# Local attention on one Trainium2 core: the mask added in four 64x64 quarter products, and the queries' copy moved ahead of the cosine product

## The reference, cut to what matters

```python
h = shift_token(x)                       # half of the channels come from the token before
q, k, v = split(h @ wqkv, 3)             # 8 heads of 64
q, k = rotary_xpos(l2norm(q) * qs, l2norm(k) * ksc)
# windows of 64 queries; each sees its own 64 keys and the 64 before them
sim = einsum('bhwid,bhwjd->bhwij', q * 8, look_around(k))
sim = where((i < j) | (i > j + 64) | (j == -1), -max, sim)
out = softmax(sim) @ look_around(v)
x = x + out @ wo                         # then a gated feed-forward layer
```

## Time and profile before

| what | value |
|---|---|
| three runs, us | 3756.16, 3765.66, 10150.55 (median 3765.66) |
| the profiled execution, us | 3774.12 |
| its span from first to last instruction, us | 3772.3 |
| mean granted TensorE clock | 0.903 |
| PE busy in the span | 2956.8 us (78%) |
| DVE, ACT, POOL busy | 2501.2, 1754.1, 1870.5 us |
| stretches of local attention, from the span's start, us | 1538 to 1807, 1929 to 2199, 2994 to 3264, 3388 to 3657 |

### The profile page before, as it was taken

One profiled execution on the slowest core, in us unless ns is written; L12 is line 12 of the kernel. 1 busy time (PEld: TensorE's weight loads), 2 busy tenths in 40 slices (PEclk: granted clock), 3 DMA queues, 4 the chain that ended last, 5 costly groups with the idle time before them and its releaser, 6 DMA issues. The chain is left out here.

```text
span 3772.3 us, 66671 instructions
## 1 busy us (share of the span) xinstructions
PE 2956.8 (78%) x21951; PEld 1709.8 (45%) x21951; DVE 2501.2 (66%) x4010; ACT 1754.1 (46%) x3307; POOL 1870.5 (50%) x1303
## 2 busy tenths in 40 slices
PE   3678456649988996799889984677677699789987
PEld 1212355523444443577557752222222377557764
DVE  5598546547766773677467744699599677557754
ACT  3543123123544544566346632444444366536652
POOL 4497221040111100788168823399199688428851
PEclk8699668668999999999999997799899899899998
DMA  3354000031112110111111110144054111101111
GB/s 83 85 161 117 8 6 7 1 95 35 34 29 40 28 28 17 34 39 37 29 27 39 38 32 8 61 158 139 29 168 161 31 40 39 33 19 40 39 34 40
DMA packets 175724, 196.54 MB, mean 52 GB/s; under 512 B 108586, under 2 KB 122752, under 8 KB 175232
## 3 DMA queue, kind: packets, MB, share of 16 engines
q1 hardware_dynamic: 175500, 193.68, 19.8%
HBM read 132.63 MB, written 9.18 MB: 38 GB/s over the span
## 5 line engine op out<-in xcount | busy, mean ns | idle before, releaser
L267 POOL TENSOR_TENSOR arena<-arena 128x1024 f32<-128x1024 f32 x192 | 451.6, 2353 | 60.5 <-DVE arena L284 33.8
L1452 DVE TENSOR_REDUCE causal_peak_parts<-psum 128x1 f32<-128x512 f32 (+3 forms) x608 | 385.1, 661 | 141.8 <-PE psum L1327 76.8
L1936 POOL TENSOR_TENSOR arena<-arena,w_minus_half 128x16 f32<-128x16 f32 x128 | 372.5, 2910 | 195.4 <-DVE arena L1858 195.3
L1435 ACT ACTIVATE arena<-psum 128x1024 f32<-128x1024 f32 (+3 forms) x352 | 294.3, 870 | 341.9 <-PE psum L1358 209.1
L1796 ACT ACTIVATE arena<-psum,arena 128x128 f32<-128x128 f32 x1024 | 277.9, 382 | 280.4 <-DVE arena L1867 280.4
L284 DVE TENSOR_TENSOR_SCAN arena<-psum,arena 128x1024 f32<-128x1024 f32 x160 | 364.6, 2279 | 27.9 <-POOL arena L267 27.8
L237 ACT ACTIVATE psum<-arena,w_A 128x1024 f32<-128x1024 f32 x192 | 214.4, 1118 | 247.8 <-DVE arena L284 210.8
L1943 POOL TENSOR_TENSOR arena<-arena 128x1024 f32<-128x1024 f32 x124 | 292.1, 2355 | 0.0
L1655 PE MATMUL psum<-w_layer_wqkv,arena 128*128 128x512 f32 x512 | 264.7, 641 | 9.1 <-ACT arena L1769 9.1
L1324 PE MATMUL psum<-arena 128*128 128x512 bf16 (+3 forms) x768 | 236.7, 348 | 39.8 <-PEq L1060 24.6
L210 PE MATMUL psum<-arena,m_sel 96*128 96x512 bf16 x384 | 117.4, 388 | 179.8 <-DVE arena L299 152.8
(11 more groups left out here) (336 smaller groups left out, 6745.4 us busy)
## 6 DMA issues: line engine op xcount, KB each, us to landing
arena<-scan_rows_large SPq DMA_DIRECT2D x128, 512.0 KB, 3.7
arena<-arena SPq DMA_DIRECT2D x256, 130.0 KB, 2.3
arena<-scan_rows_small SPq DMA_DIRECT2D x128, 256.0 KB, 3.9
arena<-causal_parts SPq DMA_DIRECT2D x288, 64.0 KB
causal_parts<-arena SPq DMA_DIRECT2D x8, 768.0 KB, 3.8
arena<-Z SPq DMA_DIRECT2D x128, 32.0 KB, 1.8
arena<-Z SPq DMA_DIRECT2D x32, 128.0 KB
arena<-Z SPq DMA_DIRECT2D x128, 28.0 KB, 1.8
```

Source lines behind the costliest of these rows:

```text
L267: pool.tensor_tensor(inputs[:, s % 2], b_lane[:, s % U], du(*runs[o]), ALU.mult).then_inc(input_up.sem, 1)
L1435: act.activation(into, place, ACT.Exp, scale=SCALE).then_inc(probs.sem, 1)
L1452: dve.tensor_reduce(part[:, heads[0]:heads[0] + len(heads), qt, half:half + 1].rearrange("p h a -> p (h a)"), place[:, 0:len(heads) * size ...
L1936: pool.tensor_tensor(RN[:, s4, :], SS[:, s4, :], k.minus_half[:, 0:2 * HEADS], ALU.pow).then_inc(rn_in.sem, 1)
```

## The change

The mask of a tile used to be one identity product of 128x128 for each of the two banks. It becomes four products of 64x64: for each half n of the queries (output partitions) and each bank r, the part r of the identity (64 input partitions) times the mask rows of half n, which now lie on input partitions of part r. The mask table in memory is laid out accordingly and is twice as large (4 x 128 instead of 2 x 128 bfloat16 per partition). Which mask form is used is known when the program is written, since TensorE's loop now goes over eight steps (`in_batches`): four steps straight, a loop of two passes over eight steps, twelve steps straight. The other engines keep their loop over four. In front of the mask products stands a semaphore increment that only holds the wait.

`turn_qk` now raises `tq_up` behind the fourth transpose (the queries are in bank 5) and `t_up` behind the eighth. `copy_q` waits for `tq_up` and stands ahead of the cosine product `rotate(i+3, 0)`.

```diff
-    sp.dma_start(mask, d["c_local"].rearrange("p (m c) -> p m c", m=2)).then_inc(loaded.sem, 16)
+    sp.dma_start(mask, d["c_local"].rearrange("p (m n c) -> p m n c", m=2, n=2)).then_inc(loaded.sem, 16)
...
-    mask = k.arena[3][:, 3584:4096].bitcast(BF16)[:, 0:2 * P].rearrange("p (m c) -> p m c", m=2)
+    mask = k.arena[3][:, 3584:4096].bitcast(BF16)[:, 0:4 * P].rearrange("p (m n c) -> p m n c", m=2, n=2)
...
+    def in_batches(eng, step, finish):
+
+        loops = (TILES - RING - AHEAD) // TPB
+        for i in range(RING):
+            step(i, i, i, AHEAD, i)
+        with eng.Fori(0, loops) as p:
+            for s in range(RING, RING + TPB):
+                step(p * TPB + s, s % RING, s % TPB, AHEAD, RING)
+        for i in range(RING + TPB * loops, TILES):
+            step(i, i % RING, i % TPB, TILES - 1 - i, RING)
+        finish(TILES - 1, (TILES - 1) % RING)
...
-                mm.then_inc(t_up.sem, 1)
-
-            def masks(i):
+                    mm.then_inc((tq_up, t_up)[m].sem, 1)
+
+            def masks(i, j):
                 pe.wait_ge(pt_in.sem, pt_in.at(i))
-                for r in range(2):
-                    o = bank[3 + r].rearrange("p (c t) -> p c t", c=PAIRS)
-                    rows = MASK[:, bass.ds((i % TPB + TPB - 1) // TPB, 1), :].broadcast_to([P, PAIRS, P])
-                    pe.matmul(o, k.identb, rows, start=True, stop=False, skip_group_check=True)
+                pe.sem_inc(held.sem, 1)
+                for n in range(2):
+                    for r in range(2):
+                        part = slice(64 * r, 64 * r + 64)
+                        o = bank[3 + r][64 * n:64 * n + 64, :].rearrange("p (c t) -> p c t", c=PAIRS)
+                        rows = MASK[part, min(j, 1), n, :].unsqueeze(1).broadcast_to([64, PAIRS, P])
+                        pe.matmul(o, k.identb[part, part], rows, start=True, stop=False, skip_group_check=True)
...
-                    masks(i + 1)
+                    masks(i + 1, (j + 1) % TPB)
...
-            in_steps(pe, step, finish)
+            in_batches(pe, step, finish)
...
             def copy_q(i, s):
-                dve.wait_ge(t_up.sem, t_up.at(i + 1))
+                dve.wait_ge(tq_up.sem, tq_up.at(i + 1))
...
-                if ahead > 2:
-                    rotate(i + 3, (s4 + 3) % RING, 0)
                 if ahead:
                     copy_q(i + 1, 1 - s)
                 if ahead > 2:
+                    rotate(i + 3, (s4 + 3) % RING, 0)
                     rotate(i + 3, (s4 + 3) % RING, 1)
```

More of the change, by code:

```diff
@@ L1542, in local_attention @@
     names = ("h_up", "h_in", "qk_up", "v_up", "v_in", "sq_in", "ss_in", "cs_in", "rn_in", "rot", "t_up", "q_in", "k_in", "s_up", "peak",
-             "probs", "pt_up", "pt_in", "o_up", "inv_in", "o_in", "ot_up", "ot_in", "y_up", "added", "ready2", "held")
+             "probs", "pt_up", "pt_in", "o_up", "inv_in", "o_in", "ot_up", "ot_in", "y_up", "added", "ready2", "held", "tq_up")
     (h_up, h_in, qk_up, v_up, v_in, sq_in, ss_in, cs_in, rn_in, rot, t_up, q_in, k_in, s_up, peak,
-     probs, pt_up, pt_in, o_up, inv_in, o_in, ot_up, ot_in, y_up, added, ready2, held) = [k.count("local_" + n) for n in names]
+     probs, pt_up, pt_in, o_up, inv_in, o_in, ot_up, ot_in, y_up, added, ready2, held, tq_up) = [k.count("local_" + n) for n in names]
     pads_in, ones_in, table_in = (k.count("local_" + n) for n in ("pads_in", "ones_in", "table_in"))
@@ L1576, in local_attention @@
     credited = (h_up, h_in, qk_up, v_up, v_in, sq_in, ss_in, cs_in, rn_in, rot, t_up, q_in, k_in, s_up, peak,
-                probs, pt_up, pt_in, o_up, inv_in, o_in, ot_up, ot_in, y_up, added, ready2)
+                probs, pt_up, pt_in, o_up, inv_in, o_in, ot_up, ot_in, y_up, added, ready2, tq_up)
     for s in credited:
@@ L1732, in _, with step @@
             pe.wait_ge(cs_in.sem, cs_in.at(2))
-            masks(0)
+            masks(0, 0)
             turn_qk(0, 0)
-            def step(i, s4, ahead, before):
+            def step(i, s4, j, ahead, before):
                 s = s4 % 2
@@ L2765, in more_constants_attention @@
     c["c_rope"] = rope.astype(f32).reshape(2, 2, TPB, P, HD).transpose(3, 2, 0, 1, 4).reshape(P, -1).copy()
-    q, kk, odd = np.arange(P)[:, None] % WIN, np.arange(P)[None], np.arange(P)[:, None] >= WIN
+    q, odd, kk = (np.arange(P) % WIN)[:, None, None], np.arange(2)[None, :, None] == 1, np.arange(P)[None, None]
     own = (kk >= WIN) == odd
     ok = np.where(own, kk % WIN <= q, kk % WIN >= q)
-    c["c_local"] = bf16(np.concatenate([np.where(ok & (own | odd), 0.0, MASKED), np.where(ok, 0.0, MASKED)], axis=1))
+    both = np.stack([ok & (own | odd), ok], axis=1)
+    c["c_local"] = bf16(np.where(both, 0.0, MASKED).reshape(P, 4 * P))
     c["c_iota"] = np.arange(SEQ, dtype=f32)
```

## The result

The changed kernel takes 3717.84 us (median of four runs, 3710.58 to 3722.09), the kernel before 3768.63 (median of 3756.16, 3765.66, 3771.60 and one run of 10150.55). Over the fast runs alone the ratio is 0.9869, with an interval of 0.9854 to 0.9884, so 1.3% faster. The forecast was 3731, and its range, 3706 to 3768, held the result; the rival "no refetch" with 3716 came nearer. The profiled executions are 3774.12 before and 3719.24 after, 54.9 apart.

What follows compares the result with a forecast made beforehand. PE's own list, pauses included, was taken to bound the local attention's step. Copy -21.6, loop edges -1.7, masks -26.7 and loop of eight +15.2 gave -34.8 us, 3731 us for a median run, range 3706 to 3768.

Steps and rivals of the forecast that it cites:

- no refetch: Rival on TensorE's loop: the eight-step body stays held, so branches cost nothing more; 3716 us, chance 0.20.
- What bounds: Local attention: PE's own list, pauses included, sets the 8.68 us step until another engine is in the way.
- Queries' copy: Ahead of turn_out: an earlier copy removes the whole 0.18 us wait in 120 steps, 21.6 us off.
- the longer steps at the loop edges: First step of each pass of the other engines' loops: 8.77 instead of 8.68, path cut, 1.7 us off.
- VectorE's reserve: Ahead of the maximum on DVE: 0.1 us is left after both gains, so moving work back costs nothing.
- sign for VectorE as the bound: In the changed trace: if the maximum starts right behind the second sine product, DVE rules and the forecast is wrong.
- Masks: Between turn_out and scores: quarter products run four side by side, 0.215 us a step, 26.7 us off over 124 steps.
- The open part of the first mask load: First load in quarter mode, ahead of the masks: open by about 0.05 us, as with the scores, and cancels.
- The pause between whole-array and quarter products: PE's list: about 0.1 us, read as the array emptying; it stays but moves from the scores to ahead of the masks.
- Loop of eight: TensorE's loop in each local attention: the longer body is not held, 4 branches back cost 15.2 us in all.
- the price of the long loop: Taken from the causal attention's loop branch, 3.7 and 5.0 us: 3.1 to 4.5 for each branch, 3.8 used.
- faster by over 2%: Whole kernel: said to need 0.6 us more a step than all terms hold; chance 0.03.

Runs made afterwards that it cites:

- e7: Whole change with TensorE's 32 steps written out without a loop, each quarter mask product made twice: step 8.47 us, attentions' sum 1045.4.
- e5: Whole change, TensorE's steps written out without a loop, queries' copy first but waiting for the eighth transpose: steps 8.43 and 8.49 us, attentions' sum 1045.8.
- e6: Whole change, TensorE's steps written out without a loop, copy waiting for the fourth transpose but behind the cosine product: steps 8.45 and 8.53 us, sum 1039.3.
- e9: Changed kernel with 128 semaphore increments ahead of each attention's work on TensorE, which moves the loop in the code: 3776.42 us, increments included.
- e8: Changed kernel with TensorE's loop of eight steps taken three times instead of twice: 3760.09 us.
- e10: Kernel before with TensorE's loop over twelve steps, taken twice, masks and copy as before: attentions' sum 1095.5 us, 21.8 more than before.
- e3: Kernel before with only TensorE's loop of eight and the mask form known when written: 3792.42 us, ratio 1.0077.
- e4: Whole change with TensorE's 32 steps written out straight instead of a loop of eight: 3710.41 us, ratio 0.9847 to the kernel before.

## Why the prediction was right, and where it was off

*What bounds.* Right. PE's list set the step and still does: it is busy 8.26 of 8.26, and a round of masks more (e7) lengthened the step by its 0.215.

*Queries' copy.* Right, with both conditions. Predicted 21.6 + 1.7, measured alone 22.3. It started 0.64 behind the first transpose where 0.65 was predicted, and the longer steps at the loop edges went. That both the order and the semaphore are needed was read from the rows, and e5 and e6 show it: each alone leaves the step at 8.43 to 8.45. (The prediction divides (1.06 - 0.27) by 8; eight products have seven gaps, and seven gives the 0.11 that it goes on with.)

*VectorE's reserve.* Right. 0.1 was predicted to be left, and the 0.69 against 0.60 behind the second sine product leaves 0.09. The prediction's sign for VectorE as the bound, a maximum right behind that product, is easily misread here, since the idle time is 0; the distance of the starts tells the two apart. With 0.215 more on PE's list the maximum came 0.215 later (e7), so PE has the last word. Between the fourth transpose and the scores PE's list can be shortened by 0.09 a step at most before VectorE's must be shortened too.

*Masks.* Mechanism right, size low: 0.215 predicted, 0.235 measured alone (8.68 to 8.45), 26.7 against 29.6 us. The open part of the first mask load was taken as 0.05, from the first score product. The first mask product is modelled as 0.40 long against 0.379 for the whole-array one, so about 0.02 is open, which would account for the difference. The pause between whole-array and quarter products moved and did not go, as predicted: 0.17 of idle time ahead of the mask loads. That it is the array emptying was read from the rows; no run tests it.

*Loop of eight.* This term was mis-sized, 15.2 predicted and 6.8 measured (7.8 at the branch itself). Its step failed where it took the price of the long loop for all four branches because 1656 loads and products lie nearer to 2225 than to 812. Only one branch missed. By its profiled body (about 1735 PE instructions with the sequencer's) it lies on the border: e9 shows that its place in the code bears on whether it is held, e8 that the place alone does not decide. A body of about 850 never missed, one of about 2540 always did (e10). The price of the one that missed was underrated too, 3.8 against 7.8: more than half of it is the second wait for instructions and the 6.8 us at half the clock, which the prediction did not have. The two errors partly cancelled, and that was luck: four branches at 7.8 would have cost 31. The Trainium skill's 2048 instructions (Runtime: NRT & Kernel Launch, Instruction fetch mechanics) agree with the trace as an upper end: a body of about 1735 can be held and one of about 2540 never was. That it fits is not enough, by e3, e8 and e9.

*The sum.* Against the profiled execution 3739.3 was predicted and 3719.2 measured, 20.1 lower: 8.4 from the loop, 3.0 from masks and copy together (53.0 in e4 against 50.0), and 8.7 from parts of the execution that the change doesn't touch. One sentence on the range is wrong: faster by over 2% would have needed 0.6 us a step in all, of which the terms hold 0.4, and not 0.6 more than they hold.

*What stays open.* Why the first branch of the first attention held in e8 and its second did not. Why some misses take the clock down and others do not. Why the unprofiled runs of e3 lie 8 to 17 us over its profiled one. Whether the straight version is faster as a whole: 3.6 us between medians is inside their scatter.

## What to carry to other kernels

An engine that is never idle in a step is its bound, and what it waits for inside its own list, like the 0.18 for the queries' copy, can come off the step in full. An identity product whose halves don't mix is worth writing in quarters: here four quarters cost the columns of one whole-array product instead of two. The pause between whole-array and quarter products does not go by that; it only changes its place. When a copy is late, look for both of its reasons, the semaphore it waits for and what stands ahead of it in its queue: here neither helped alone. And when a loop body grows, count its instructions: an eight-step loop that was held or missed by a shift of 128 instructions, at about 7 us a miss, ate nearly the whole gain when it was taken three times.

## What the runs showed of the hardware

Products of 64x64 in bfloat16 with 512 columns run four side by side in the four quarters: four more cost 0.215 us, the time of one whole-array product's columns at 2.4 GHz.

A taken loop branch on TensorE took 0.21 to 0.23 us when the target was still held, 3.3 to 5.0 when it was not, and the fall-through 0.08. Behind a miss a second wait for instructions can follow (0.9 to 3.0 us here). In 14 of the 16 misses in the local attention the granted clock then fell from 1.00 to 0.50, in the changed kernel for 6.8 us; one miss cost 3.2 to 3.3 us where the clock stayed up (e10) and 4.8 to 8.9 where it fell.

On VectorE a row's length is not the distance to the next: behind a 128x512 product of 0.68 us the next one starts 0.60 later when nothing else holds it (e5).
